# Group norm's sums taken with the residual, x normalised on GpSimd, maxima turned as fp32r, and a plan with landing times

## The chip, the cores and the metric

The kernel runs on one core of one Trainium2 chip. The metric is device time in microseconds (us). Three runs of the kernel before gave 111.69, 111.75 and 113.16 us, median 111.75. One more execution was profiled; all rows below are from it.

## What is computed

The input x has shape 2 x 128 x 16 x 16: a batch of 2, with 128 channels (C) and 256 tokens (T). Four attention blocks run one after the other, and each takes the x that the one before gave:

```
h = group_norm(x, 32 groups of 4 channels x 256 tokens) * gn_w + gn_b
q, k, v = wq h + bq, wk h + bk, wv h + bv
p = softmax(q k^T * scale)        # blocks 0 to 2: 8 heads of 16; block 3: 1 head of 128
x = x + wp (p v) + bp
```

## The kernel before

The whole problem lives in SBUF. Channels are the 128 partitions and tokens the free dimension, so each of the two samples (b = 0 and 1) is one 128x256 tile, `xs0` or `xs1`. The work is cut into steps named (kind, block l, sample b, index i). `step_needs` lists what each step waits for. `plan_order` is a list scheduler: from a table of costs (`STEPS`, `ONE_HEAD_STEPS`), landing times of the first transfers (`LANDED`) and priorities (`LEAD`, `FAVOURED`) it makes one order of all steps and gives each a PSUM bank, of which there are eight. Each engine then runs its own steps in that order, strictly one after the other, and waits on semaphores for the others. So the numbers in the tables decide which instruction stands behind which, and nothing at run time does.

One block of several heads runs like this for each sample:

- Group norm. DVE takes the moments of x (`bn_stats` over 256 tokens, `bn_aggr`, and two operations on one column, L622 to L625). TensorE averages them over the groups (`group_means`, L412 and L414), DVE forms the variance (L630), GpSimd raises it to the power -1/2 (`rsqrt`, L356), and DVE normalises x into `hn` (L633).
- Projections on TensorE: two of q and two of k (each serves a set of four heads, L431) and one of v (L438). ACT and DVE split q and k into parts in fp32r (a format of 32 bits that TensorE takes in one pass, where fp32 needs two instructions): L555, L560, L645, L650. GpSimd extends k (L352).
- Scores in four steps of two heads (`scores`, L451); DVE takes the negative row maxima (`row_max`, L666) into columns of `neg_max`. `turn_max` (L466 and L469) turns a set's maxima into rows by a product with the identity, and ACT stores them in `q_max` (L580).
- Scores again with keys as rows (`scores_t`, L483), `exps` on ACT (L584), `attend` on TensorE (L495), which also gives the sums. ACT stores that (L599), TensorE turns it (`turn_out`, L517), DVE divides (L683, L688), TensorE turns it back (`turn_back`, L525), DVE adds the bias of v (`att`, L661), `project_out` (L532), and DVE adds the residual into `xs` (L701).

Block 3 has one head and half as many operations. Before each block's projections its weights are scaled by gn_w (`scale_w`, L549) and gn_b is folded into the biases (`fold_bias`, ten weight loads with a matmul of one column each, L423 and L424; then `add_bias` on DVE, L640).

The plan also puts fillers on TensorE (`warm`, a 128x128 fp32 product of zeros, L406), where by its own reckoning the engine would do too little in a while. It counts each as 0.222 us, at any time of the program. In the order before there are 24: 16 in the head and 8 at the ends of blocks 0 to 2. The first transfers go out from two queues: SP's has x of sample 0, the weights of block 0, x of sample 1 and then the other weights; ACT's has the constants and the vectors.

The lines of `turn_max`, for the types:

```
mm(dst[:, 0:T], only_high[:, :], q_split[b][:, i, :], start=True, stop=False)          # L466, fp32r
pe.wait_ge(max_done, nth("row_max", l, b, PER * (i + 1) - 1))
for qc in range(NCH):
    last = mm(dst[:, qc * CHUNK:(qc + 1) * CHUNK], neg_max[b][:, i, qc, :], ident, ...)  # L469, fp32
```

Of the kernel before, what the change touches and what calls it, by code (L numbers as in the profile page):

```python
# [46 lines left out]
    "moments": ("V", .95, 1.1), "group_means": ("P", .3, .6), "variance": ("V", .25, .4),  # L47
    "rsqrt": ("G", .56, .65), "normalise": ("V", .4, .6), "project_q": ("P", .43, .65), "project_k": ("P", .43, .65),
    "mask_q": ("A", .47, .65), "split_q": ("V", .41, .6), "round_k": ("A", .4, .56), "split_k": ("V", .41, .6),
    "extend_k": ("G", .7, .8), "project_v": ("P", .45, .65), "store_v": ("A", .32, .5),  # L50
    "scores": ("P", .5, .68), "row_max": ("V", .6, .78), "turn_max": ("P", .57, .8), "store_max": ("A", .32, .5),
    "scores_t": ("P", .5, .68), "exps": ("A", .495, .7), "attend": ("P", .9, 1.1), "store_out": ("A", .32, .5),
    "turn_out": ("P", .25, .45), "divide": ("V", .5, .65), "turn_back": ("P", .25, .45),
    "store_attended": ("V", .41, .6), "project_out": ("P", .5, .7), "residual": ("V", .41, .6),
}
ONE_HEAD_STEPS = {
# [9 lines left out]
LANDED = {("moments", 0, 0, 0): 3.5, ("scale_w", 0, 0, 0): 4.9, ("group_means", 0, 0, 0): 4.4,  # L66
          ("moments", 0, 1, 0): 5.6}
# [4 lines left out]
LEAD = [17, 5, 5, -14]  # L72
FAVOURED = {"attend": -33, "normalise": 26, "exps": -22, "turn_max": 22, "store_out": 35, "scores": -14, "scores_t": -13, "row_max": -13, "store_max": 21}


def cost(step):

    return ONE_HEAD_STEPS.get(step[0], STEPS.get(step[0])) if step[1] == MULTI else STEPS[step[0]]


EMPTIED_BY = {"fold_bias": "add_bias", "group_means": "normalise", "project_q": "split_q", "project_k": "split_k",
              "project_v": "store_v", "turn_max": "store_max", "attend": "store_out", "turn_out": "divide",
              "turn_back": "store_attended", "project_out": "residual"}
EMPTIED_BY_ONE_HEAD = {"fold_bias": "add_bias", "group_means": "normalise", "project_q": "scale_q",
# [78 lines left out]
def plan_order():  # L163
# [18 lines left out]
    while len(done) < len(needs):  # L182
        best = None
        for step in needs:
# [11 lines left out]
            rank = (start, -way(step) - LEAD[l] * (b == 0) - FAVOURED.get(kind, 0.))  # L196
# [3 lines left out]
        engine, busy, later = cost(step)  # L200
        starts[step] = start
        free[engine] = start + busy
# [8 lines left out]
    for step in sorted((s for s in starts if cost(s)[0] == "P"), key=starts.get):  # L211
        t = max(begin + busy for begin, busy, _ in work[-1:])
        while t + WARM <= starts[step] - MARGIN * (warm > 0 and t > 6.):
            active = sum(share * max(0., min(begin + busy, t) - max(begin, t - WINDOW)) for begin, busy, share in work)
            spare = [n for n in range(BANKS)
                     if all(to <= t or begin >= t + 2 * WARM for begin, to in taken[n])]
            if active < ENOUGH * WINDOW and spare:
                filler = "warm", 0, 0, warm
                starts[filler], banks_of[filler] = t, spare[:1]
                work.append((t, WARM, 1.))  # L220
                warm += 1
            t += WARM
        work.append((starts[step], cost(step)[1], ROWS_USED.get(step[0], 1.) if step[1] < MULTI else 1.))
# [3 lines left out]
def attention_blocks(nc: bass.Bass, x, out, vectors, constants, weights):  # L227
# [10 lines left out]
    with ExitStack() as ctx:  # L238
# [17 lines left out]
        minus_half = const[:, HALF_COL:HALF_COL + 1]  # L256
        blank, blank_exp = sb("blank", [C, C]), sb("blank_exp", [C, 1])
        only_high = sb("only_high", [C, C], F32R)

        bn = [sb(f"bn{b}", [C, 6]) for b in range(B)]  # L260
        mom = [sb(f"mom{b}", [C, 5]) for b in range(B)]
        grp = [sb(f"grp{b}", [C, 2]) for b in range(B)]
# [7 lines left out]
        neg_max = [sb(f"neg_max{b}", [C, SETS, NCH, C]) for b in range(B)]  # L270
# [27 lines left out]
        only_high_ready = sem("only_high_ready")  # L298
        vchain = sem("vchain")
        warm_ready = sem("warm_ready")  # L300
# [43 lines left out]
        def _(pool):  # L344
            for b in range(B):
                nc.gpsimd.memset(neg_max[b][:, :, :, :], 0.0).then_inc(max_zeros_ready, 1)
                nc.gpsimd.memset(v_heads[b][:, :, :, :], 1.0).then_inc(v_ones_ready, 1)
            pool.wait_ge(const_in, 16)
            for kind, l, b, i in order:
# [4 lines left out]
                elif kind == "rsqrt":  # L354
                    pool.wait_ge(variance_ready, nth("variance", l, b))
                    nc.gpsimd.tensor_tensor(grp[b][:, 1:2], grp[b][:, 0:1], minus_half,  # L356
                                            ALU.pow).then_inc(rsqrt_ready, 1)

        @block.tensor
        def _(pe):  # L360
            mm = nc.tensor.matmul

            def bank_free(step, j=0):
# [6 lines left out]
                elif emptier[0] == "normalise":  # L370
                    pe.wait_ge(h_ready, nth(*emptier))
# [27 lines left out]
            for step in order:  # L399
# [7 lines left out]
                elif kind == "group_means":  # L407
# [4 lines left out]
                    mm(m[:, 0:3], group_avg, const[:, EPS_COL + 3 * l:EPS_COL + 3 * (l + 1)], start=True, stop=False)  # L412
                    pe.wait_ge(moments_done, nth("moments", l, b))
                    mm(m[:, 0:3], group_avg, mom[b][:, 0:5:2], start=False, stop=True).then_inc(means_done, 1)  # L414
# [46 lines left out]
                elif kind == "turn_max":  # L461
                    if l == b == i == 0:
                        pe.wait_ge(only_high_ready, 1)
# [4 lines left out]
                    for qc in range(NCH):  # L468
                        last = mm(dst[:, qc * CHUNK:(qc + 1) * CHUNK], neg_max[b][:, i, qc, :], ident,  # L469
# [133 lines left out]
        def _(dve):  # L603
# [10 lines left out]
            for step in order:  # L614
                kind, l, b, i = step
                multi = l < MULTI
                if kind == "moments":
                    if l == 0:
                        dve.wait_ge(x_in[b], 16)
                    else:  # L620
                        dve.wait_ge(x_ready, nth("residual", l - 1, b))
                    link(nc.vector.bn_stats(bn[b][:, :], xs[b][:, :]))  # L622
                    link(nc.vector.bn_aggr(mom[b][:, 0:2], bn[b][:, :]))
                    ts(mom[b][:, 2:3], mom[b][:, 0:1], -1.0, None, ALU.mult)
                    stt(out=mom[b][:, 4:5], in0=mom[b][:, 0:1], scalar=mom[b][:, 0:1], in1=mom[b][:, 1:2],  # L625
                        op0=ALU.mult, op1=ALU.add).then_inc(moments_done, 1)
# [4 lines left out]
                elif kind == "normalise":  # L631
# [130 lines left out]
```

## Time and profile before

| | before |
|---|---|
| median of 3 runs | 111.75 us (111.69 to 113.16) |
| the profiled execution: its time | 111.87 us |
| its span, first to last instruction | 110.1 us |
| TensorE busy | 97.5 us, 89% |
| DVE busy | 70.8 us, 64% |
| ACT busy | 55.2 us, 50% |
| GpSimd busy | 13.1 us, 12% |
| mean granted TensorE clock | 0.984 |

The time is 1.8 us more than the span. PE is TensorE's matmuls, PEld its weight loads, POOL is GpSimd, SP the engine that starts most transfers. A matmul's row gives it until its last result is out, and the next begins before that; what one costs in a stream is the distance from one start to the next. An fp32 matmul stands as two instructions in the profile. The average of a busy share mixes the head, where nothing can be computed yet, with the blocks, so the stretches are read one by one.

### The profile page before, as it was taken

Reading aid. Unit: us, or ns where it says so; the run is one execution under the profiler, and the core shown is the slowest. Engines: PE = TensorE matmul, PEld = TensorE weight load, DVE = VectorE, ACT = ScalarE, POOL = GpSimd, SP = SyncE. Lnnn points to the kernel's source line nnn. Section 1 sums busy time; section 2 is a strip of 40 time slices with the busy share of each in tenths; the row PEclk is TensorE's granted clock in tenths of the full one; section 3 lists DMA queues with packets and bytes.
Section 4 is the critical chain, followed back from the end, with each engine's and each line's share of the span. In section 5 each row is a group of like instructions: output and inputs, shape, how many; then the busy total and the mean of one; then the engine's idle time right before and its main releaser. Section 6 shows DMA issues by size and latency. Waiting matters only on the chain.

```text
span 110.1 us, 2481 instructions
## 1 busy us (share of the span) xinstructions
PE 97.5 (89%) x932; PEld 75.3 (68%) x932; DVE 70.8 (64%) x188; ACT 55.2 (50%) x124; POOL 13.1 (12%) x28
## 2 busy tenths in 40 slices
PE   0299999999999689999999978999999988896991
PEld 0299987978664578779857437878886644776860
DVE  0130578998713769988871176899898027677662
ACT  4300075659596107087359840618757892025620
POOL 7000242220000013222000001052200000110000
PEclk9999999999999999999589999999999999999999
DMA  2970000000000000000000000000000000000011
GB/s 63 337 271 5 0 0 6 0 0 0 9 0 0 0 0 6 0 3 0 6 0 0 6 0 0 0 0 0 6 0 0 6 0 0 0 3 0 6 48 48
DMA packets 1739, 2.28 MB, mean 21 GB/s; under 512 B 320, under 2 KB 1216, under 8 KB 1728
## 3 DMA queue, kind: packets, MB, share of 16 engines
q1 hardware_dynamic: 1440, 1.97, 5.4%
q8 instruction: 8, 0.13, 0.5%
q10 hardware_dynamic: 288, 0.16, 0.5%
q14 instruction: 3, 0.02, 0.1%
HBM read 1.86 MB, written 0.26 MB: 19 GB/s over the span
## 4 chain that ended last, share of the span: by engine, by line
PE 76%; ACT 8%; DVE 6%; DMA 3%; issue 3%; ACTq 0%; DVEq 0%
PE ps L431 11%; PE ps L451 10%; PE ps L495 9%; PE ps L483 9%; ACT probs L584 6%; PE ps L406 6%; PE ps L532 5%; PE ps L469 5%; PE ps L423 4%; DMA vec<-in_vectors 3%; PE ps L438 3%; PE ps L466 3%; PE ps L517 2%; ACT o_raw L599 2%; PE ps L503 2%
## 5 line engine op out<-in xcount | busy, mean ns | idle before, releaser
L666 DVE TENSOR_REDUCE neg_max<-ps 128x2 f32<-128x512 f32 x48 | 30.5, 684 | 1.4 <-PE ps L451 1.3
L584 ACT ACTIVATE probs<-ps 128x512 f32<-128x512 f32 x48 | 25.8, 604 | 6.5 <-PE ps L483 6.4
L555 ACT ACTIVATE q_low<-ps,bias_low,const 128x256 fp32r<-128x256 f32 x12 | 6.8, 565 | 23.7 <-PE ps L431 23.6
L431 PE MATMUL ps<-hn,ws 128*128 128x256 f32 x56 | 14.5, 390 | 1.0 <-issue 0.9
L495 PE MATMUL ps<-probs,v_heads 128*32 128x256 f32 x192 | 13.4, 398 | 0.2 <-ACT probs L584 0.2
L483 PE MATMUL ps<-q_split,k_high 32*128 32x256 f32 x96 | 13.0, 330 | 0.1
L451 PE MATMUL ps<-k_high,q_split 32*128 32x256 f32 x96 | 12.2, 337 | 0.1
L431 PEld LDWEIGHTS ps<-hn,ws 128*128 128x128 f32 x56 | 9.8, 189 | 3.2 <-issue 1.7
L356 POOL TENSOR_TENSOR grp<-grp,const 128x1 f32<-128x1 f32 x8 | 4.4, 552 | 61.4 <-DVE grp L630 61.4
L483 PE MATMUL ps<-q_max,k_ext 32*128 32x256 f32 x96 | 11.1, 281 | 0.0
L451 PE MATMUL ps<-k_low,q_split 32*128 32x256 f32 x96 | 10.9, 292 | 0.0
L683 DVE RECIPROCAL rden<-ps 128x8 f32<-128x8 f32 x12 | 2.5, 206 | 13.0 <-PE ps L517 13.0
L483 PEld LDWEIGHTS ps<-q_split,k_high 32*128 32x128 f32 x96 | 8.5, 187 | 3.2 <-issue 1.9
L451 PEld LDWEIGHTS ps<-k_high,q_split 32*128 32x128 f32 x96 | 8.7, 197 | 1.8 <-issue 1.1
L352 POOL TENSOR_SCALAR k_ext<-k_low,const 128x256 fp32r<-128x256 f32 x12 | 6.7, 558 | 23.9 <-DVE k_low L650 23.9
L423 PE MATMUL ps<-vec,w 128*128 128x1 f32 x32 | 5.0, 277 | 4.9 <-DMA vec<-in_vectors 4.9
L406 PE MATMUL ps<-blank 128*128 128x128 f32 x48 | 9.1, 342 | 0.0
L451 PEld LDWEIGHTS ps<-k_low,q_split 32*128 32x128 f32 x96 | 8.9, 202 | 0.0
L483 PEld LDWEIGHTS ps<-q_max,k_ext 32*128 32x128 f32 x96 | 8.6, 190 | 0.0
L495 PEld LDWEIGHTS ps<-probs,v_heads 128*32 128x32 f32 x192 | 5.2, 113 | 4.8 <-issue 1.7
L423 PEld LDWEIGHTS ps<-vec,w 128*128 128x128 f32 x32 | 4.7, 225 | 5.2 <-DMA vec<-in_vectors 4.9
L406 PEld LDWEIGHTS ps<-blank 128*128 128x128 f32 x48 | 8.0, 250 | 0.0
(61 smaller groups left out, 147.5 us busy)
## 6 DMA issues: line engine op xcount, KB each, us to landing
w<-in_w SPq DMA_DIRECT2D x3, 384.0 KB, 5.2
xs<-in_x SPq DMA_DIRECT2D x2, 128.0 KB, 3.1
w<-in_w SPq DMA_DIRECT2D x1, 256.0 KB, 5.8
out<-xs SPq DMA_DIRECT2D x4, 64.0 KB, 1.5
const<-in_constants ACTq DMA_DIRECT2D x1, 136.0 KB, 2.9
vec<-in_vectors ACTq DMA_DIRECT2D x1, 16.0 KB, 3.7
```

The source lines that it names most:

```text
L352: nc.gpsimd.tensor_scalar(k_ext[b][:, i, :], k_low[b][:, i, :].bitcast(F32), high_rows, one_row, ALU.mult, ALU.add).then_inc(k_extended, 1)
L406: mm(slot(*step)[:, 0:C], blank[:, :], blank[:, :], start=True, stop=True)
L423: mm(dst[:, at + s:at + s + 1], w[l][:, first + s * multi, :], beta, start=True, stop=True)
L431: mm(slot(*step)[:, 0:T], ws[l][:, block_of[l] + i, :], hn[b][:, :], start=True, stop=True).then_inc(done, 1)
L451: last = mm(slot(*step, j)[:, qc * T:(qc + 1) * T], q_split[b][r:r + QUAD, s, qc * CHUNK:(qc + 1) * CHUNK], keys[b][r:r + QUAD, s, :], sta ...
L469: last = mm(dst[:, qc * CHUNK:(qc + 1) * CHUNK], neg_max[b][:, i, qc, :], ident, start=False, stop=(qc == NCH - 1))
L483: last = mm(slot(*step, j)[:, kc * T:(kc + 1) * T], part[b][r:r + QUAD, s, keys], queries[b][r:r + QUAD, s, :], start=(n == 0), stop=(n == 1))
L495: last = mm(slot(*step)[QUAD * j:QUAD * (j + 1), 0:T], v_heads[b][:, kc, h, :], probs[b][:, h, kc, :], start=(kc == 0), stop=(kc == NCH - 1))
L532: mm(slot(*step)[:, 0:tokens], w[l][:, W_P[l], :], att[b][:, i * CHUNK:i * CHUNK + tokens], start=True, stop=True).then_inc(out_projected, 1)
L555: nc.scalar.activation(q_low[b][:, i, :], slot("project_q", l, b, i)[:, 0:T], ACT.Identity, bias=bias_low[:, l, i:i + 1], scale=low_rows). ...
L584: nc.scalar.activation(probs[b][:, i, :, :].rearrange("p c t -> p (c t)"), slot("scores_t", l, b, i // PACK, i % PACK)[:, :], ACT.Exp, sca ...
L666: nc.vector.tensor_reduce(neg_max[b][:, i // PER, :, QUAD * (i % PER) + MAX_ROW], slot("scores", l, b, i // PACK, i % PACK)[:, :].rearrang ...
```

## The change

**Sums in place of moments.** `bn_stats` and `bn_aggr` go, with the two operations on one column. The residual's instruction now also sums x along the tokens (`accum_out`), and one more pass squares x and sums the squares. For block 0, where no residual stands ahead, a first pass sums x. The division by 4 x 256 moves into the constant `group_avg`; a matmul of one column with `minus_avg` (made on GpSimd once) gives the negative mean. So the group's mean, its negative and the mean square stand in the same three PSUM columns as before.

**Normalising on GpSimd.** DVE copies the mean out of PSUM behind the variance (`mean_ready`), and GpSimd normalises x right behind its own rsqrt. The PSUM bank is free once the mean is copied.

**Maxima in fp32r.** `neg_max` and the identity (`ident_r`) are fp32r, so L469's product is one instruction instead of two.

**The plan.** It has new costs and priorities for every kind, its own landing times, and reckons TensorE's steps (fillers too) at twice their cost until 6.5 us. In this early stretch it fills every gap. The whole order follows from that.

```diff
+COLD_UNTIL = 6.5
-LEAD = [17, 5, 5, -14]
-FAVOURED = {"attend": -33, "normalise": 26, "exps": -22, ...
+LEAD = [896.5, -85.3, -422.8, -819.6]
+FAVOURED = {"add_bias": 112.1, "attend": -105, "divide": -244.4, "exps": -68, ...
+def cost_at(step, start):
+    engine, busy, later = cost(step)
+    cold = busy if engine == "P" and start < COLD_UNTIL else 0.
+    return busy + cold, later + cold
...
-        while t + WARM <= starts[step] - MARGIN * (warm > 0 and t > 6.):
+        while True:
+            spent = WARM * (2 if t < COLD_UNTIL else 1)
+            if t + spent > starts[step] - MARGIN * (t > COLD_UNTIL):
+                break
...
-            if active < ENOUGH * WINDOW and spare:
+            if (t < COLD_UNTIL or active < ENOUGH * WINDOW) and spare:
...
+                elif kind == "normalise":
+                    pool.wait_ge(rsqrt_ready, nth("rsqrt", l, b))
+                    pool.wait_ge(mean_ready, nth("variance", l, b))
+                    nc.gpsimd.tensor_scalar(hn[b][:, :], xs[b][:, :], grp[b][:, 1:2], grp[b][:, 2:3],
+                                            ALU.subtract, ALU.mult).then_inc(h_ready, 1)
...
+                    mm(m[:, 1:2], minus_avg[:, :], mom[b][:, 0:1], start=False, stop=False)
                     pe.wait_ge(moments_done, nth("moments", l, b))
-                    mm(m[:, 0:3], group_avg, mom[b][:, 0:5:2], start=False, stop=True).then_inc(means_done, 1)
+                    mm(m[:, 0:3], group_avg, mom[b][:, :], start=False, stop=True).then_inc(means_done, 1)
...
-                        last = mm(dst[:, qc * CHUNK:(qc + 1) * CHUNK], neg_max[b][:, i, qc, :], ident,
+                        last = mm(dst[:, qc * CHUNK:(qc + 1) * CHUNK], neg_max[b][:, i, qc, :], ident_r[:, :],
...
+                        link(stt(out=squares[b][:, :], in0=xs[b][:, :], scalar=0.0, in1=xs[b][:, :], op0=ALU.mult,
+                                 op1=ALU.add, accum_out=mom[b][:, 0:1]))
...
-                    link(nc.vector.bn_stats(bn[b][:, :], xs[b][:, :]))
-                    link(nc.vector.bn_aggr(mom[b][:, 0:2], bn[b][:, :]))
-                    ts(mom[b][:, 2:3], mom[b][:, 0:1], -1.0, None, ALU.mult)
-                    stt(out=mom[b][:, 4:5], in0=mom[b][:, 0:1], scalar=mom[b][:, 0:1], in1=mom[b][:, 1:2],
-                        op0=ALU.mult, op1=ALU.add).then_inc(moments_done, 1)
+                    stt(out=squares[b][:, :], in0=xs[b][:, :], scalar=1.0, in1=xs[b][:, :], op0=ALU.mult,
+                        op1=ALU.mult, accum_out=mom[b][:, 2:3]).then_inc(moments_done, 1)
...
-                elif kind == "normalise":
-                    dve.wait_ge(rsqrt_ready, nth("rsqrt", l, b))
-                    ts(hn[b][:, :], xs[b][:, :], slot("group_means", l, b)[:, 0:1], grp[b][:, 1:2], ALU.subtract,
-                       ALU.mult).then_inc(h_ready, 1)
+                    ts(grp[b][:, 1:2], m[:, 0:1], 1.0, None, ALU.mult).then_inc(mean_ready, 1)
```

The order of instructions moves on every engine; two places of TensorE's order show how. In these rows `blank` marks a filler, `vec,w` is `fold_bias`, `const` and `mom` are `group_means`, and `hn,ws` or `ws,hn` are the projections. The first place is the head of TensorE's program, here in the kernel before.

```order
L423 MATMUL ps<-vec,w 128x1 x4
L424 MATMUL ps<-vec,w 128x1
L406 MATMUL ps<-blank 128x128 x10
L412 MATMUL ps<-const 128x3
L414 MATMUL ps<-mom,const 128x3
L406 MATMUL ps<-blank 128x128 x6
```

After the last of these rows there is a second pair of L412 and L414 for sample 1, and then the first projection. This is the same place in the changed kernel.

```order
L438 MATMUL ps<-blank 128x128 x8
L444 MATMUL ps<-const 128x3
L450 MATMUL ps<-mom,minus_avg 128x1
L452 MATMUL ps<-mom,const 128x3
L461 MATMUL ps<-vec,w 128x1 x4
L462 MATMUL ps<-vec,w 128x1
L469 MATMUL ps<-hn,ws 128x256 x4
```

The fillers now stand ahead of all else, eight of them. Sample 0's means come before `fold_bias`, and between that and the projections nothing is left; sample 1's means have moved behind the projections of sample 0.

The second place is the end of block 0. Here `probs,v_heads` is `attend` for one set of four heads, `o_raw` is `turn_out`, `o_tok` is `turn_back`, and `att,w` is `project_out`. TensorE's rows of the kernel before, from the last `attend` of sample 1 to the first projections of block 1:

```order
L495 MATMUL ps<-probs,v_heads 32x256 x8
L532 MATMUL ps<-att,w 128x256
L517 MATMUL ps<-const,o_raw 128x128 x4
L412 MATMUL ps<-const 128x3
L414 MATMUL ps<-mom,const 128x3
L406 MATMUL ps<-blank 128x128
L525 MATMUL ps<-const,o_tok 128x128 x2
L406 MATMUL ps<-blank 128x128 x2
L532 MATMUL ps<-att,w 128x256
L431 MATMUL ps<-hn,ws 128x256 x4
```

And of the changed kernel, from the last `attend` of sample 1 to the first scores (`k_high,q_split`) of block 1:

```order
L533 MATMUL ps<-probs,v_heads 32x256 x8
L555 MATMUL ps<-const,o_raw 128x128 x4
L469 MATMUL ps<-hn,ws 128x256 x2
L563 MATMUL ps<-const,o_tok 128x128 x2
L469 MATMUL ps<-hn,ws 128x256 x2
L476 MATMUL ps<-ws,hn 128x128 x2
L570 MATMUL ps<-att,w 128x256
L489 MATMUL ps<-k_high,q_split 128x256 x2
```

Sample 0's `project_out` and means have moved ahead of these rows, in among the second scores and the `attend` steps of sample 1. Block 1's projections for sample 0 now surround sample 1's `turn_back` and `project_out` instead of following them. There are no fillers in this place; four stand later in block 1, ahead of sample 1's projections. The ends of blocks 1 and 2 moved in the same way but less: only one projection goes ahead of sample 1's `project_out`, and it stands behind `turn_back`. Altogether the changed order has 12 fillers.

## Rows read from the trace of the kernel before

**Rows 1.** The page: busy time of each engine, share of the span, instructions

```profile
PE 97.5 (89%) x932; PEld 75.3 (68%) x932; DVE 70.8 (64%) x188; ACT 55.2 (50%) x124; POOL 13.1 (12%) x28
```

**Rows 2.** Windows: stretch, length, busy PE PEld DVE ACT POOL, granted clock, DMA, GB/s

```profile
0.00:13.54 13.54, 8.64 (x51) 8.64 (x51) 3.05 (x14) 2.31 (x3) 2.67 (x9) 1.00 0.42 137
13.54:34.63 21.09, 20.61 (x238) 15.69 (x237) 15.22 (x33) 15.38 (x34) 2.79 (x5) 1.00 0.01 2
34.63:40.41 5.78, 4.36 (x37) 3.19 (x38) 3.59 (x13) 0.66 (x3) 0.55 (x1) 1.00 0.00 0
40.41:64.15 23.74, 23.24 (x244) 17.51 (x243) 16.75 (x38) 15.61 (x34) 2.74 (x5) 0.93 0.01 2
64.15:68.83 4.68, 4.04 (x35) 2.65 (x35) 3.37 (x12) 0.40 (x2) 0.55 (x1) 1.00 0.00 0
68.83:91.22 22.39, 22.03 (x244) 16.90 (x243) 16.65 (x38) 15.51 (x34) 2.74 (x5) 1.00 0.01 1
```

**Rows 3.** The chain of waits in the head: start us, us, what

```profile
1.16 3.69 DMA vec<-in_vectors
...
4.90 1.86 PE ps L423 x8
6.76 0.43 PE ps L424 x2
7.19 4.34 PE ps L406 x20
...
11.87 1.44 PE ps L406 x12
```

**Rows 4.** The timeline of the head: start us, us, engine, line, operation, [idle before]

```profile
0.72 0.38 SPq L330 DMA_DIRECT2D xs<-in_x  x1
0.82 0.17 DVE L612 MEMSET blank<- 128x128 f32 x1 [0.82 <-PEq L756]
...
11.91 0.29 DVE L630 TENSOR_SCALAR grp<-ps 128x1 f32<-128x1 f32 x1 [3.40 <-PE ps L414]
...
12.35 0.56 POOL L356 TENSOR_TENSOR grp<-grp,const 128x1 f32<-128x1 f32 x1 [9.72 <-DVE grp L630]
```

**Rows 5.** The tile xs: issue to landing of its two loads, least, median, most

```profile
DMA to landing us min/median/max: 2.7/3.1/3.4
```

**Rows 6.** The chain at the end of block 0: start us, us, what

```profile
35.76 0.64 PE ps L532 x2
...
38.88 0.42 PE ps L525 x2
```

**Rows 7.** Groups by form: busy us, mean ns of one, idle before

```profile
L352 POOL TENSOR_SCALAR k_ext<-k_low,const 128x256 fp32r<-128x256 f32 x12 | 6.7, 558 | 23.9 <-DVE k_low L650 23.9
L599 ACT ACTIVATE o_raw<-ps 128x256 f32<-128x256 f32 x12 | 4.8, 398 | 5.9 <-PE ps L495 5.9
L701 DVE SCALAR_TENSOR_TENSOR xs<-ps,vec,xs 128x256 f32<-128x256 f32 x6 | 2.9, 483 | 2.8 <-PE ps L532 2.8
L589 ACT ACTIVATION_READ_ACCUMULATOR p_one<-ps,neg_max_one 128x1 f32 x4 | 0.8, 196 | 0.0
```

**Rows 8.** The timeline of TensorE at one turn_max

```profile
29.80 0.39 PE L466 MATMUL ps<-q_split,only_high 128*128 128x256 f32 x1
30.02 0.61 PE L469 MATMUL ps<-const,neg_max 128*128 128x128 f32 x4
30.47 0.38 PE L517 MATMUL ps<-const,o_raw 128*128 128x128 f32 x2
```

**Rows 9.** Windows in block 1: TensorE busy, and its granted clock ahead of DMA

```profile
52.00:53.00 1.00, 1.00 (x16) 0.88 (x19) 0.96 (x4) 0.89 (x3) 0.00 (x0) 0.61 0.00 0
...
55.00:56.00 1.00, 1.00 (x16) 0.28 (x8) 1.00 (x3) 0.65 (x2) 0.00 (x0) 0.69 0.00 0
```

**Rows 10.** Two attend steps, block 1 and block 0: start us, us

```profile
28.18 1.00 PE ps L495 x16
...
54.53 1.55 PE ps L495 x16
```

## The prediction: what the change should do to the time

> **What bounds the kernel now.** I read the busy table first: TensorE is busy 89% of the span and nobody else over 64% [rows 1]. That is an average, so I cut the span with the windows view at the places where the program changes character [rows 2]. The reader should see three kinds of stretch. The head lasts 13.54 us and ends with the first projection. A block has an inner stretch of 21.1 to 23.7 us, from its first projection to its last exponential, in which TensorE is busy 98% and DVE and ACT some 70%. Between blocks lie 4.7 to 5.8 us in which TensorE has fillers and gaps: the last attend of sample 1 has to become x again, and that takes every engine in turn. The stretch between blocks 2 and 3 is as long as the one between 1 and 2, 4.68 us.
>
> Then the chain of waits in the head [rows 3]. It waits for the vectors until 4.85, runs `fold_bias` from 4.90 to 7.19 (1.86 and 0.43) and then goes through 20 instructions of fillers in 4.34 us. [...] The plan believed 0.222 each and put ten in front of sample 0's means. x of sample 0 had landed at 0.72 + 2.7 = 3.4 us [rows 4, 5]. So some 4 us of the head is filler that real work waited behind, and DVE too had put the bias ahead of the moments. The head is this kernel's largest single loss.
>
> **Part 1, the head.** The changed order has eight fillers first. They can start when `blank` is set, at 0.82 + 0.17 = 0.99 [rows 4], and end at 0.99 + 8 x 0.434 = 4.46. DVE's two passes over x of sample 0 start at 3.4. No row shows a summing pass of DVE with both inputs in SBUF. The nearest is the residual, the same operation on 128x256, 0.48 us; ACT's accumulator costs 0.20 more in an instruction of its own [rows 7]. So a pass is 0.48 to 0.68; I take 0.48, and the moments are there at 4.5 (4.9 at the upper end). Sample 0's means are three small matmuls of two instructions; none is dearer than a filler's two, 0.43. The last of them stands behind the moments, so the means are there at about 5.3. From there two things run side by side. [...] On the other side, variance to the start of rsqrt is 12.35 - 11.91 = 0.44, rsqrt 0.56 [rows 4], normalising on GpSimd 0.56 by the one operation of its form and size there, `k_ext` [rows 7], and about 0.15 for each of the hops: 5.3 + 0.44 + 0.56 + 0.56 + 0.3 = 7.2. [...] First projection 7.2 to 7.6, at worst 8.0; I take 7.5 against 13.54: **-6.0 us**. The scaled weights are no obstacle: ACT needs under a microsecond after the vectors' 4.85.
>
> Sample 1's two passes stand in DVE's order ahead of the bias; its x took 3.4 us from issue to landing [rows 5], so they too are done before `fold_bias` is.
>
> **Part 2, the end of block 0.** Before, from the last exponential to the next projection it takes 5.78 us [rows 2]. `project_out` of sample 0 stands behind the last attend, at 35.76 [rows 6], so DVE gets sample 0's residual and moments just when sample 1's divisions should start, and `turn_back` starts only at 38.88. In the changed order `project_out` of sample 0 goes ahead, among the second scores. The path left is attend 1.00 [rows 10], ACT's store 0.40 [rows 7], `turn_out` 0.38 [rows 8] and two hops, 0.2: first projection after about 2.0. But `turn_back` (0.42) and `project_out` (0.64) of sample 1 [rows 6] now run inside block 1, and its four fillers, 0.24 each [rows 3], show that sample 1's norm comes late there. I count them in full, 1.0. 5.8 - 2.0 - 1.06 - 1.0 = **-1.8 us** with the rounding (5.78, 0.96).
>
> **Part 3, the ends of blocks 1 and 2.** Here sample 1's tail keeps its serial path through `turn_back` and `project_out`, and only sample 0's norm is out of its way: a shorter chain on DVE, and one projection ahead of `project_out`. From 4.68 I take off 0.3 each: **-0.6 us**. The bound below is nothing; above, that of part 2.
>
> **Part 4, the maxima in fp32r.** One `turn_max` takes 0.22 (one fp32r instruction of 256 columns) and then 0.45 for four fp32 instructions of 128 columns, start to start [rows 8]. Two are left. No row shows an fp32r product of 128 columns with 128 rows. If each costs as much as the one of 256 columns, 0.22, nothing is saved; if as much as one fp32 pass, 0.11, 0.23 is saved; if half of that, 0.34. I take 0.23 (the loads of 128 rows are still there), so 12 x 0.23 = 2.8 us of TensorE's time. Inside a block TensorE is busy 98%, but DVE and ACT, at 15 to 17 us of 21 to 24 [rows 2], limit in parts, where the gain turns into waiting. I count 0.7 of it: **-2.0 us**, bounds 0 and -4.1.
>
> **Part 5, the rest at nothing.** DVE loses the moments' four operations and the normalising, and gains a squaring pass and a copy of one column, under 0.3 as the variance's is [rows 4]. The difference relieves DVE a little, which TensorE's busy 98% hides; if that cover is gone, it is a gain. `group_means` gains two small instructions, 0.1 us each eight times, partly in gaps. GpSimd has 12% load [rows 1], so eight more of 0.56 find room; what is queued behind them is `extend_k`, which is needed only after the first maxima.
>
> **Sum.** The profiled execution took 111.87, its span 110.1; the median of the runs, 111.75, is the same within 0.1%. 111.9 - 6.0 - 1.8 - 0.6 - 2.0 = **101.5 us**. I keep the one stretch at the lower clock in block 1 (below) as it is.
>
> **A rule against the change.** In this trace `k_ext` on GpSimd takes 558 ns at each of its twelve places, while DVE works alongside, and no DVE operation of size there reads two inputs from SBUF [rows 7]. The new squaring passes do, and they can meet a normalising. If a normalising had to wait for one whole pass each time, up to 0.48 us eight times would be lost, of which the first is covered by `fold_bias`. [...] No row here shows it either way. Most squaring passes stand in DVE's order ahead of the norm that waits for them, so they meet the other sample's `k_ext` rather than a normalising.
>
> **Rivals.**
> - *Only the head.* The new order's ends of blocks bring nothing, because sample 1's tail is just moved into the next block, and the fp32r product is no cheaper. Then 111.9 - 6.0 = 105.9. For it speaks that I have not seen an fp32r product of this shape. Against it, the gaps between blocks are there in the windows.
> - *The lock.* GpSimd's normalising waits for DVE as above: 101.5 + 3.4 = 104.9.
> - [...] In block 1 the granted clock falls between 52 and 56 us [rows 9], and the same sixteen instructions of attend take 1.55 instead of 1.00 [rows 10]. The mean of 0.93 over 23.74 us [rows 2] makes that 1.7 us. Before it TensorE did scores on 32 rows and the one-column matmuls of `fold_bias`. The change halves the fillers, from 24 to 12, and thins `turn_max`. Two more such stretches give 101.5 + 3.4 = 104.9. Without any it would be 99.8, and with TensorE's full saving of part 4 it would be 97.7.
> [...]
> - *The change does nothing*, because the fillers ahead of the real work were covering a late transfer. x at 3.4 and the vectors at 4.85 exclude that for the head.
>
> **How the numbers follow.** The forecast 0.58, only the head 0.12, the lock 0.08, more stretches at 1.2 GHz 0.10, a better one (no lower clock, the full saving of part 4) 0.08, the two last rivals together 0.04. The range goes from 97.7, the better case, to 105.5, which takes in the lock and two more stretches at the lower clock; "only the head" and the last two stay outside, 0.16. A measurement of this kernel can tell some 2% from no change, that is 109.5 to 114.0. The last two rivals, at about 112, are nearly all "same": faster 0.96, same 0.03, slower 0.01.
>
> **What would show it.** In the profile after: first projection at 7.2 to 7.6 us (part 1); from the last exponential of block 0 to block 1's first projection about 2 us, and that of blocks 1 and 2 still 3.9 to 4.4 (parts 2, 3); the product of `neg_max` at about 0.11 an instruction, start to start, two instead of four (part 4); normalising at 0.56 on GpSimd, without outliers (the lock); one stretch with a granted clock under 1 (the clock). The prediction is wrong if the first projection stands later than 8.5, or if the inner stretches grow by what the ends lost.

## The result, and the profile after

| | before | changed |
|---|---|---|
| median of 5 runs | 111.75 us | 113.35 us (113.06 to 117.56) |
| ratio, 95% interval | | 1.0135 [1.0098, 1.0172] |
| span, profiled execution | 110.1 us | 113.4 us |
| DVE busy | 70.8 us | 67.1 us |
| GpSimd busy | 13.1 us | 23.9 us |
| mean granted TensorE clock | 0.984 | 0.925 |

The forecast was 101.5 us, in a range from 97.7 to 105.5. The changed kernel is 1.4% slower than before. The executions scatter: three lie near 113, and the profiled one, which all lines below are from, took 115.34 at nearly the same mean clock (0.925 against 0.923), so no trace shows what the 2 us between them are.

Two lines of the changed kernel's page. The second gives the granted clock in 40 slices of the span (9 is full speed, 5 is half); before, all but two slices showed 9:

```profile
PE 99.3 (88%) x900; PEld 76.5 (67%) x900; DVE 67.1 (59%) x183; ACT 55.5 (49%) x124; POOL 23.9 (21%) x39
PEclk9999985999999999999999999997555999995999
```

The windows of the changed kernel, cut at the same events as [rows 2] (columns as there) and carried on through the end of block 2 and block 3. For the last two, the kernel before has these:

```profile
91.22:95.90 4.68, 3.82 (x34) 2.43 (x34) 3.37 (x12) 0.39 (x2) 0.55 (x1) 1.00 0.00 0
95.90:110.10 14.20, 10.75 (x61) 8.34 (x59) 8.79 (x29) 4.90 (x16) 0.55 (x1) 1.00 0.07 20
```

And the changed kernel:

```profile
0.00:8.59 8.59, 6.99 (x32) 6.93 (x33) 2.89 (x15) 2.31 (x3) 4.78 (x13) 1.00 0.65 217
8.59:35.09 26.50, 24.53 (x238) 19.21 (x238) 16.50 (x37) 15.82 (x34) 3.99 (x6) 0.94 0.01 2
35.09:38.13 3.04, 2.45 (x26) 1.40 (x26) 1.24 (x6) 0.72 (x3) 1.78 (x2) 1.00 0.00 0
38.13:61.06 22.93, 21.71 (x248) 16.66 (x248) 16.81 (x40) 14.95 (x34) 3.99 (x6) 1.00 0.01 2
61.06:65.52 4.46, 2.69 (x28) 1.69 (x29) 2.65 (x11) 0.67 (x3) 1.78 (x2) 1.00 0.01 4
65.52:92.36 26.84, 25.25 (x238) 18.63 (x238) 15.99 (x37) 15.10 (x34) 3.97 (x6) 0.81 0.01 1
92.36:96.81 4.45, 2.73 (x30) 1.69 (x29) 2.68 (x11) 0.66 (x2) 1.78 (x2) 1.00 0.00 0
96.81:113.40 16.59, 12.96 (x64) 10.33 (x64) 8.35 (x28) 5.24 (x16) 1.78 (x2) 0.90 0.06 16
```

The head did give 4.95 us (13.54 to 8.59) and the end of block 0 2.7. The two other ends gave 0.2 each. But block 0's inner stretch grew from 21.1 to 26.5, block 2's from 22.4 to 26.8, and block 3 from 14.2 to 16.6; only block 1's became shorter, by 0.8. In the blocks TensorE is busy 93 to 95% in place of 98%, and the granted clock in block 2 is 0.81.

The groups by form show the instruction at fault, of the changed kernel (L388 normalises, L379 is `k_ext`):

```profile
L388 POOL TENSOR_SCALAR hn<-xs,grp 128x256 f32<-128x256 f32 x8 | 9.9, 1232 | 0.8
L379 POOL TENSOR_SCALAR k_ext<-k_low,const 128x256 fp32r<-128x256 f32 x12 | 6.6, 555 | 15.7 <-DVE k_low L686 15.7
```

Same engine, same size, both a `tensor_scalar` with two operations: 1.23 us against 0.56. The chain of the changed kernel shows who waits for it, and what comes then (L469 are projections, L504 and L507 `turn_max`):

```profile
8.46 0.14 issue
8.59 3.75 PE ps L469 x8
...
14.81 1.23 POOL hn L388
16.05 0.09 issue
16.14 2.63 PE ps L469 x6
...
22.33 0.32 PE ps L504
22.64 0.17 PE ps L507 x2
```

The first eight projection instructions take 3.75 us; in the kernel before the same eight took 1.84. In x0_forms below the same eight took 3.75 where the record gives a granted clock of 0.50 (8.54 to 12.30), so 3.75 is the time at half the full clock, though the record of the changed kernel says 1.00 there. From 15.0 to 16.1 TensorE stands still for sample 1's normalising, and the next six take 2.63. The windows around that stop, of the changed kernel:

```profile
15.00:16.00 1.00, 0.01 (x1) 0.00 (x0) 1.00 (x3) 0.00 (x0) 1.00 (x1) 1.00 0.00 0
16.00:17.00 1.00, 0.86 (x3) 0.78 (x4) 1.00 (x3) 0.00 (x0) 0.04 (x1) 0.71 0.00 0
17.00:18.00 1.00, 1.00 (x4) 0.82 (x3) 1.00 (x2) 0.47 (x1) 0.00 (x0) 0.50 0.00 0
```

### The profile page after: what moved, and what is told of

The parts are those of the page before. It is cut to its first block, busy times and chain, and to the rows that moved or that the text cites. A ratio compares the mean times of both kernels' runs of the same rounds, so it can differ in the third digit from the quotient of the medians.

```text
span 113.4 us, 2434 instructions
## 1 busy us (share of the span) xinstructions
PE 99.3 (88%) x900; PEld 76.5 (67%) x900; DVE 67.1 (59%) x183; ACT 55.5 (49%) x124; POOL 23.9 (21%) x39
## 3 DMA queue, kind: packets, MB, share of 16 engines
q1 hardware_dynamic: 1440, 1.97, 5.2%
HBM read 1.86 MB, written 0.26 MB: 19 GB/s over the span
## 4 chain that ended last, share of the span: by engine, by line
PE 79%; issue 6%; ACT 6%; POOL 3%; DVE 3%
PE ps L469 16%; PE ps L533 11%; PE ps L489 10%; PE ps L521 10%; ACT probs L622 5%; PE ps L438 4%; PE ps L476 4%; PE ps L570 4%; PE ps L555 2%; PE ps L504 2%; POOL hn L388 2%; PE ps L461 2%; PE ps L452 2%; PE ps L541 2%; PE ps L497 2%
## 5 line engine op out<-in xcount | busy, mean ns | idle before, releaser
L702 DVE TENSOR_REDUCE neg_max<-ps 128x2 fp32r<-128x512 f32 x48 | 30.0, 685 | 8.1 <-PE ps L489 8.1
L469 PE MATMUL ps<-hn,ws 128*128 128x256 f32 x56 | 19.1, 479 | 7.0 <-issue 5.3
L469 PEld LDWEIGHTS ps<-hn,ws 128*128 128x128 f32 x56 | 12.2, 235 | 10.1 <-issue 8.5
L598 ACT ACTIVATE k_high<-ps,bias 128x256 fp32r<-128x256 f32 x12 | 5.5, 474 | 22.7 <-PE ps L469 22.7
L489 PE MATMUL ps<-k_high,q_split 32*128 32x256 f32 x96 | 11.9, 335 | 0.5 <-ACT probs L622 0.3
L521 PE MATMUL ps<-q_split,k_high 32*128 32x256 f32 x96 | 10.8, 344 | 1.2 <-ACT q_max L618 1.1
L388 POOL TENSOR_SCALAR hn<-xs,grp 128x256 f32<-128x256 f32 x8 | 9.9, 1232 | 0.8
L379 POOL TENSOR_SCALAR k_ext<-k_low,const 128x256 fp32r<-128x256 f32 x12 | 6.6, 555 | 15.7 <-DVE k_low L686 15.7
L637 ACT ACTIVATE o_raw<-ps 128x256 f32<-128x256 f32 x12 | 4.7, 393 | 10.4 <-PE ps L533 10.4
L521 PE MATMUL ps<-q_max,k_ext 32*128 32x256 f32 x96 | 9.4, 293 | 0.0
L686 DVE SCALAR_TENSOR_TENSOR k_low<-ps,bias,k_high 128x256 fp32r<-128x256 f32 x12 | 5.4, 480 | 3.4 <-ACT k_high L598 3.4
L697 DVE TENSOR_SCALAR att<-ps,bias 128x256 f32<-128x256 f32 (+1 forms) x10 | 4.3, 430 | 4.7 <-PE ps L563 3.7
```

The source lines that it names most:

```text
L379: nc.gpsimd.tensor_scalar(k_ext[b][:, i, :], k_low[b][:, i, :].bitcast(F32), high_rows, one_row, ALU.mult, ALU.add).then_inc(k_extended, 1)
L388: nc.gpsimd.tensor_scalar(hn[b][:, :], xs[b][:, :], grp[b][:, 1:2], grp[b][:, 2:3], ALU.subtract, ALU.mult).then_inc(h_ready, 1)
L469: mm(slot(*step)[:, 0:T], ws[l][:, block_of[l] + i, :], hn[b][:, :], start=True, stop=True).then_inc(done, 1)
L489: last = mm(slot(*step, j)[:, qc * T:(qc + 1) * T], q_split[b][r:r + QUAD, s, qc * CHUNK:(qc + 1) * CHUNK], keys[b][r:r + QUAD, s, :], sta ...
L521: last = mm(slot(*step, j)[:, kc * T:(kc + 1) * T], part[b][r:r + QUAD, s, keys], queries[b][r:r + QUAD, s, :], start=(n == 0), stop=(n == 1))
L598: nc.scalar.activation(k_high[b][:, i, :], slot("project_k", l, b, i)[:, 0:T], ACT.Identity, bias=bias[:, l, K_BIAS + i:K_BIAS + i + 1]).t ...
```

## The experiments

Times are medians of four executions with their range, and the kernel before on the same chip beside them. Different groups of variants ran on different chips. The theory: the subtract form on GpSimd is slow, and the stops that it causes and the fp32r product lower the clock. The rivals: the new order itself, and the removed fillers.

### What a tensor_scalar costs on GpSimd

```diff
 # abridged
+ for op0, op1 in (subtract, mult), (add, mult), (mult, add), (mult, subtract), (mult, mult), ...
+     nc.gpsimd.tensor_scalar(probe, hn[0], one_row, high_rows, op0, op1)   # unused, one after the other
```

> The changed kernel with ten more tensor_scalar operations on GpSimd after its last normalising, each on 128 partitions with per-partition scalars, waiting for one another: subtract then mult, add then mult, mult then add, mult then subtract, mult then mult (256 columns, fp32 out), subtract then mult and mult then add with fp32r out, a single mult, and subtract then mult and mult then add on 128 columns. They compute nothing that is used. Theory (the pair of operations sets GpSimd's price): the mult-then-add forms take 0.55 us like k_ext, and those that begin with subtract 1.22, whatever the output type. Rival (the operand sets it, since the normalising reads scalars from a tile just written, or its output is fp32): all forms with fp32 output take 1.22, or all of them 0.55. On 128 columns a slow form should cost about 0.65, since the price goes with the columns.

The timeline of GpSimd in this kernel, the second, third and fourth form:

```profile
107.43 0.55 POOL L410 TENSOR_SCALAR probe<-hn,const 128x256 f32<-128x256 f32 x1
108.08 0.56 POOL L410 TENSOR_SCALAR probe<-hn,const 128x256 f32<-128x256 f32 x1
108.73 1.23 POOL L410 TENSOR_SCALAR probe<-hn,const 128x256 f32<-128x256 f32 x1
```

Subtract then mult took 1.25 and mult then subtract 1.23; add-mult, mult-add and mult-mult 0.55 to 0.56. A subtract in either place doubles the price. With fp32r output subtract-mult took 1.23 and mult-add 0.67; `k_ext`, which is such a mult-add, takes 0.56, so that difference stays open. A single mult took 0.93, more than two operations. On 128 columns it was 0.80 against 0.45: I had expected 0.65 for the slow form, and the price does not halve with the columns. The whole kernel took 120.71 in this one execution. That is not the probes' time: they end at 115.2 beside block 3, the chain that ended last does not go through them, and the granted clock was 0.841.

### The normalising on DVE, and on GpSimd with an add

```diff
-nc.gpsimd.tensor_scalar(hn, xs, mean, rstd, ALU.subtract, ALU.mult)
+nc.vector.tensor_scalar(hn, xs, mean, rstd, ALU.subtract, ALU.mult)          # x1_dve
+nc.gpsimd.tensor_scalar(hn, xs, minus_mean, rstd, ALU.add, ALU.mult)         # x4_add; the copy takes column 1
```

> The changed kernel with the normalising back on DVE, at the same place of the same order. [...] Rival (the clock falls because fillers were taken out, not because of the gaps): 108 to 110 with a granted clock of still about 0.92. Rival (the new order is bad inside the blocks): 109 or more with a high clock.

> The changed kernel with one form exchanged: the copy takes the negative mean out of PSUM, and GpSimd normalises with add and mult in place of subtract and mult. Same result, same order. Theory (the subtract form is what made the normalising 1.23 us; add then mult took 0.55 in the probe): eight normalisings of 0.56, time like the one with the normalising on DVE or a little under, 103 to 106 us, the path shorter by 0.67 at five to seven of them and the clock lower less often. [...]

On DVE: 106.48 (104.52 to 107.23) against 112.63, ratio 0.934 [0.922, 0.946]; I had expected 102 to 106. With the add on GpSimd: 106.44 (104.33 to 106.67) against 112.01. The changed kernel itself has 113.35 against 111.75. The eight normalisings of the second, by its line:

```profile
L388 POOL TENSOR_SCALAR hn<-xs,grp x8: 553/554/618, 7.2 to 93.7; 128x256 f32<-128x256 f32 x8
```

One ALU name is worth 7 us of 113.4. Eight times 0.67 us are only 5.4, and not all of that is on the path; the granted clock also rose, to 0.967 to 0.984 from 0.92. How the 7 us divide between the two is not measured. Which engine normalises does not matter (106.48 and 106.44).

The mean granted clock is not the whole account either. On DVE the two executions at 1.00 took 107.0 and 107.2, and those at 0.984 and 0.967 took 105.9 and 104.5. In the profiled one (107.23) TensorE's durations are still the long ones until after 13.5 us (eight instructions of `fold_bias` in 1.85, eight of the projections in 3.76), where the record shows 1.00; the others have no trace.

### Fillers where TensorE waits

```diff
# four fillers ahead of each sample's first projection in each block, one ahead of the first of all
+if step[0] == "project_k" and step[3] == 0:
+    order.append(filler)
```

> The changed kernel, with four fillers ahead of each sample's first projection in each block (one in the first place), 29 more in all, in the bank of that projection. They stand where TensorE waits for the normalising. Theory (TensorE's clock falls because TensorE stands still there): the granted clock rises from 0.92 to 0.97 or more, and the time falls by 3 to 5 us, to 108 to 110, though every normalising is as slow as before. Rival (the clock does not hang on these gaps): granted clock stays at 0.92, time same or up to 2 us longer.

110.9, between 107.41 (clock 0.984) and 115.45 (0.895), against 112.63; ratio 0.958 [0.946, 0.969]. I had expected 108 to 110 at 0.97 or more. The two best executions, 107.41 and 108.43, had clocks of 0.984 and 1.00 and are 5 to 6 us under the changed kernel with every normalising as slow as before. None of the changed kernel's nine executions was above 0.939. So the clock can be had back by work where TensorE stops, and the slow form alone, with the clock high, costs little: 107.41 against 106.44 with the add. But the two others, 113.37 (0.939) and 115.45, gained nothing, so the fillers there do not secure the clock.

### The head alone, and fp32r maxima in it

```diff
 # the kernel before, with new landing times only (x3_head, x11_head_again)
-LANDED = {("moments", 0, 0, 0): 3.5, ..., ("group_means", 0, 0, 0): 4.4, ("moments", 0, 1, 0): 5.6}
+LANDED = {("moments", 0, 0, 0): 3.7, ..., ("fold_bias", 0, 0, 0): 4.9, ("moments", 0, 1, 0): 5.7}
 # and in addition (x7_head_r)
-mm(dst[...], neg_max[b][:, i, qc, :], ident, ...)
+mm(dst[...], neg_max[b][:, i, qc, :], ident_r, ...)      # both fp32r
 # and in addition (x10_r_fill): one filler ahead of each turn_max
```

> The kernel before with nothing changed but the plan's landing times, so that fillers come first, sample 0's means come ahead of fold_bias, and the moments ahead of the bias: the head alone. [...] Rival (an earlier start only runs into the lower clock, and gives it back): under 2 us gained.

> The head-only variant once more, on the chip of the others here, since it was measured on another chip than its fp32r version. Theory: 105 to 108, granted clock 0.97 or more, as before, so the 9.5 us between the two are the fp32r maxima. Rival (the difference was the chip): 113 or so here.

> The head-only variant of the kernel before (new landing times only), with the maxima written and turned as fp32r in addition, in the same order. Theory (0.28 us less in each of twelve turn_max steps, most of them on the path): 1.5 to 3 us under the head-only variant's 105.6, so 102.6 to 104. Rival (inside the blocks DVE and ACT hold the path): under 0.5 us, 105 or more; or the clock falls more often because TensorE has less to do.

> The head-only variant with fp32r maxima, which took 113.2 to 117.3 at a granted clock of 0.87, with one filler (two fp32 instructions of 128 columns, 0.22 us) ahead of each of the twelve turn_max steps. That puts back roughly the TensorE time that fp32r had saved, in another place and with useless work. Theory (the clock hangs on how much TensorE does, and fp32r took it below what it takes): clock back to 0.96 or more and 105 to 108. Rival (fp32r products themselves, or their type, lower the clock): 113 or more, granted clock below 0.9.

| | us | before | ratio | granted clock |
|---|---|---|---|---|
| x3_head | 105.62 (105.36 to 107.9) | 112.63 | 0.936 [0.929, 0.944] | 0.965 to 0.983 |
| x11_head_again | 106.11 (105.84 to 106.39) | 112.18 | 0.949 [0.945, 0.953] | 0.983 to 0.984 |
| x7_head_r | 115.01 (113.2 to 117.25) | 112.01 | 1.016 [1.005, 1.026] | 0.852 to 0.874 |
| x10_r_fill | 107.07 (106.64 to 107.24) | 112.18 | 0.957 [0.953, 0.961] | 0.966 to 0.967 |

The head alone takes off 6 to 7 us, more than the 4 to 5 that I expected here and about what part 1 said. Adding fp32r maxima, with all else in place, adds 9; twelve fillers that do nothing useful take 8 of these back. So it is not the fp32r products as such that lower the clock. Of x3_head, three windows:

```profile
10.00:14.50 4.50, 4.50 (x46) 3.50 (x44) 4.19 (x9) 3.06 (x7) 1.22 (x3) 1.00 0.00 0
14.50:17.80 3.30, 3.08 (x35) 2.59 (x34) 3.10 (x7) 1.47 (x4) 0.39 (x2) 1.00 0.02 5
17.80:27.80 10.00, 9.85 (x144) 6.95 (x143) 6.11 (x14) 8.34 (x20) 0.50 (x1) 1.00 0.01 2
```

And the same of x7_head_r, its fp32r version:

```profile
10.00:14.50 4.50, 4.50 (x46) 3.51 (x45) 4.33 (x9) 3.06 (x7) 1.34 (x3) 1.00 0.00 0
14.50:17.80 3.30, 3.26 (x36) 2.71 (x37) 3.30 (x7) 1.47 (x5) 0.67 (x2) 1.00 0.02 5
17.80:27.80 10.00, 10.00 (x100) 7.24 (x100) 5.30 (x12) 6.55 (x15) 0.19 (x1) 0.50 0.01 2
```

The two run alike until 14.5 us. Then come two `turn_max` steps, 0.28 us shorter each, and scores on 32 rows; from 17.8 on the second has a granted clock of 0.50 for 10 us and starts 100 matmuls where the first starts 144. Between 14.5 and 17.8 the second was busy 3.26 us of 3.30, more than the first with 3.08, so a stop is not what lowered its clock. It fell in all four executions (0.852 to 0.874 as a mean) and not in those of x10_r_fill, which put fp32 work back. So the clock can fall without a stop, where fp32 work is taken out. Whether fillers in fp32r would hold it as well was not tried.

With the fillers of x10_r_fill the granted clock was 0.966 in place of 0.87. But work without a stop did not always bring the clock up: in x13_full_r below TensorE was busy for all of 1.04 to 13.57 us, and from 10.37 on its eight projection instructions still took 3.43 us, for 1.85 in the chains of x3_head and x10_r_fill.

### Maxima back in fp32 in the changed kernel

> The changed kernel with GpSimd's normalising in the add-then-mult form and the maxima back in fp32 (two products of four instructions), same order. Compared with the same kernel with fp32r maxima (106.44, 104.3 to 106.7). Theory (the faster product costs the clock more than it saves): the clock stays at 0.98 or more in all executions and the time is no longer, 103 to 106, though TensorE has 12 x 0.28 = 3.4 us more to do. Rival (in this order the work is dense enough for fp32r, only the other order suffers): 107 to 109.

> The changed kernel with only the maxima back in fp32; the normalising stays slow. Theory (fp32r maxima share in the changed kernel's low clock): granted clock above 0.95 instead of 0.92, time 109 to 112. Rival (the gaps from the slow normalising alone pull the clock down): clock still about 0.92, and 114 to 116, by the 3.4 us of work added.

With the fast normalising: 105.17 (104.03 to 108.06) against 106.44 with fp32r, 1.3 us less, within the scatter, though TensorE has 3.4 us more to do. The clock did not stay at 0.98 in all executions, as I had expected: it was 0.936 to 1.00. With the slow one: 113.05 (110.14 to 118.5) against 112.18 before. Its two best, 110.1 and 110.3, give the ratio 0.985 [0.980, 0.991] at a clock of 0.969, and its two others took 115.8 and 118.5 at 0.925 and 0.912; the changed kernel has 111.53 to 119.19 over all its executions. So in the new order fp32r maxima save nothing that can be measured. That they share in the changed kernel's miss is likely by the best executions, but not shown; in any case they cost far less there than the 9 us of the old order.

### The clock in the head

```diff
 # in words; the first fillers stand ahead of sample 0's means, the others ahead of the first projection
+x5_eleven, x6_both (with the add): three more fillers at the start
+x12_full, x13_full_r (with the add; maxima fp32 and fp32r): one more at the start, four ahead of the projection
```

> The changed kernel with three more fillers in its head, eleven instead of eight, and nothing else. [...] Rival (the clock in the head is a matter of phase and not of the fillers' number): no change, 113.

> The changed kernel with both: add and mult on GpSimd, and eleven fillers in the head. [...] Rival (the new order also loses inside the blocks): 104 or more with a granted clock above 0.97.

> The kernel with add-then-mult on GpSimd and fp32 maxima (105.17 before), with one more filler at the start (nine) and four ahead of the very first projection, where TensorE stood still for 1.0 us. [...]

> The same fillers with fp32r maxima. Theory: as the one with fp32 maxima or up to 2 us less, since TensorE has 3.4 us less to do, 101 to 104, but with a lower granted clock in some executions. Rival (fp32r maxima cost clock in this order too): 105 or more, granted clock under 0.96.

> The changed kernel itself, on the chip of these two, since the variants were measured on other chips than it. All theories expect 113 to 118 with a granted clock of 0.92; a time under 110 would mean that the variants' gains were partly the chip's.

Eleven fillers alone did not help: 116.32 (114.19 to 120.17) for the changed kernel, where I had expected 109 to 111, and 106.24 (105.54 to 113.42) with the add, the same as with eight and not the 101 to 103 expected. x12_full took 104.64 (102.44 to 106.72) against 111.57, expected 102 to 103.5. Eight instructions of its `fold_bias` took 0.89 us, where the chain of the kernel before has 1.86; its chain:

```profile
1.04 4.21 PE ps L451 x18
...
5.98 0.89 PE ps L474 x8
```

What the fillers in the stop did is seen beside x8_add_f32, the same kernel without them and with one filler fewer at the start. TensorE's timeline of x8_add_f32, `fold_bias` and then the first projections:

```profile
5.27 1.03 PE L461 MATMUL ps<-vec,w 128*128 128x1 f32 x8
6.16 0.36 PE L462 MATMUL ps<-vec,w 128*128 128x1 f32 x2
7.44 3.57 PE L469 MATMUL ps<-hn,ws 128*128 128x256 f32 x8 [0.91 <-POOL hn L388]
```

And of x12_full:

```profile
5.84 1.03 PE L474 MATMUL ps<-vec,w 128*128 128x1 f32 x8
6.74 0.36 PE L475 MATMUL ps<-vec,w 128*128 128x1 f32 x2
6.96 1.14 PE L451 MATMUL ps<-blank 128*128 128x128 f32 x8
8.01 1.97 PE L482 MATMUL ps<-hn,ws 128*128 128x256 f32 x8
```

In both, eight instructions of `fold_bias` took 1.03 us; in the changed kernel they took 1.84. After the stop of 0.91 us the eight projection instructions take 3.57, at a granted clock of 0.53 (7.44 to 11.02), and with fillers in its place 1.97; I had expected about 1.85. Three more profiles of the new order (x0_forms, x6_both, x9_f32) had `fold_bias` in 1.03 and then a stop, of 0.91 to 1.58 us; their projections took 2.82 to 3.75. But the whole kernel gained only 0.5 us by it, within the scatter.

x13_full_r took 108.34 (102.89 to 113.4), expected 101 to 104. In its profile TensorE worked without a stop from 1.04 us on, and the first projections still took 3.43, for 1.85 in the chain of x3_head:

```profile
6.32 1.71 PE ps L474 x8
8.03 0.43 PE ps L475 x2
8.45 1.92 PE ps L451 x8
10.37 3.43 PE ps L482 x8
```

So in these profiles filling the stop kept a clock that had risen, and did not make it rise. When it rises is not settled: in the four profiles of the old order with the new head it had risen ahead of `fold_bias`, by 5.3 to 6.2 us (`fold_bias` took 1.03 for eight instructions); in the new order in five profiles of twelve, with nearly the same instructions at the start. In the other seven `fold_bias` took 1.84 or 1.85 and the first projections 3.62 to 3.76, in some with no stop between them. The changed kernel itself gave 114.2 (111.53 to 119.19) on this chip, against 111.57; the chip is not the reason.

## Why the prediction was wrong, step by step

- **The signs.** I had named two signs of being wrong, and both came: the first projection stands at 8.59, later than 8.5, and the inner stretches of blocks 0 and 2 grew by 5.4 and 4.5, more than the ends lost.
- **What bounds the kernel, and the head: right.** The two head-only runs gave -7.0 and -6.1 for the predicted -6.0. In the changed kernel the first projection came at 8.59, outside the 7.2 to 8.0. The fillers ended at 4.82 for 4.46, and the three small matmuls ran behind them one after the other, so the means were there at 5.9 and not at 5.3; and the normalising took 1.29 for 0.56. The passes of DVE were well sized: 0.43, and 0.08 for the sum. The 7.6 at the upper end of my sum is the 5.3 and `fold_bias` at its 2.29 of before: it took 2.27 in the changed kernel (5.75 to 8.02), and 1.26 in x12_full (5.84 to 7.10).
- **The step that failed: "normalising on GpSimd 0.56 by the one operation of its form and size there".** The form was not the same. `k_ext` is a mult and an add, the normalising a subtract and a mult, and that is 1.23. This term should have come from a row for the same pair of operations, or been open upwards. Part 5 then called eight of them free. With the add in place of the subtract the kernel takes 106.44 in place of 113.35, so this step holds 7 of the 11.9 us missed, with what it did to the clock.
- **The rival on the clock was mis-sized.** I named it by a frequency, which no run here shows; what the runs show of such a stretch is a granted clock of 0.50 (x7_head_r, 17.80 to 27.80). I gave it 0.10, and priced two more stretches at 1.7 us each. By the mean of 0.925 over 113.4 us the changed kernel lost an estimated 8.5 us of full clock, before 1.8 (0.016 of 110.1). The head comes on top, where the record says 1.00 and eight projection instructions took 1.9 us too long. This overlaps with the step above: the slow form's stops are one cause of it. I saw that fillers and fp32 work were taken out and did not ask what the old fall in [rows 9] had hung on.
- **Part 4: the size right, the sign wrong.** Two instructions in 0.17 for four in 0.45 save 0.28 each, inside the bounds. But the time did not fall by it: +9 in the old order, by way of the clock, and in the new one no gain (106.44 against 105.17 without it), where I had -2.0.
- **Part 2 and 3: the mechanism right, the gain mostly absent.** 3.0 us from the last exponential to the first projection of block 1, 4.5 for the others. The 0.67 too much per normalising is in both; with the fast form x12_full has 2.4 and 3.8, for the predicted 2.0 and 3.9 to 4.4. But beside x3_head, with the old order and the new head, x12_full's profile is only 1.0 us shorter (102.7 against 103.7): the three ends are shorter by 5.1 together, the inner stretches longer by 1.8, the head by 0.7 and block 3 by 1.7 (15.9 against 14.2). Block 3 was at nothing in my sum. Its granted clock is 0.89 in x12_full and 0.90 in the changed kernel. By an estimate, 0.11 of 15.9 us is 1.7, the whole growth.
- **"Only the head" is nearly what came, once the faults are out.** I gave it 0.12, at 105.9. By the medians, head-only took 0.938 and 0.946 of the time of the kernel before on its chip, and x8_add_f32 and x12_full 0.938 both. The new order thus brings 1 us at most beyond its head, where I had -2.4 for parts 2 and 3.
- **The lock: its case did not arise.** In the trace no squaring pass ran beside a normalising. Two ran beside sample 0's rsqrt in the head (6.20 to 7.08), and it took 0.74 for 0.56, 0.2 more and not a whole pass. The first normalising took 1.29 for 1.22, but beside DVE's `only_high` and `ident_r`, which read one tile. What a normalising would lose beside such a pass, no run here shows; the whole pass of 0.48 each, 3.4 us in all, was my estimate.
- **The last two rivals: the number near by chance.** I had put them at about 112, and 113.35 came. But the head did give 4.95 us, and block 0's inner stretch had a granted clock of 0.94, so TensorE was not at half the full clock all through it.

With the add, fp32 maxima and the fillers in the head, x12_full has a median of 104.64 and a best of 102.44. That is inside the range, but 3 us above the forecast: 2.0 of them are part 4, which is not in x12_full, and about as much is what block 3 lost by the clock. Why the clock falls there is open.

## What to carry to other kernels

Take the price of an operation from a row with the same ALU operations, not only the same engine and size; where there is none, probe it. In a kernel whose TensorE is the bound, do not count less work on it as a gain in itself (x7_head_r, with less of it, took 115.01 for x3_head's 105.62): look at the granted clock around the places where work is removed, and keep fillers there until a run shows that they can go. The safest version here is the kernel before with new landing times, 105.4 to 107.9 over eight executions. The best single execution is x12_full's, 102.44, but its median against the kernel before is the same, 0.938.

## What the hardware did that I had not expected

- On GpSimd a tensor_scalar with a subtract took 1.22 to 1.25 us for 128x256 in fp32, with add and mult in any order 0.55 to 0.56, and a single mult 0.93 (x0_forms).
- TensorE's granted clock fell to 0.50 with its busy share at 0.99 to 1.00 (x7_head_r, 17.80 to 27.80), after nothing but 0.56 us of fp32 work was taken out of the stretch ahead.
- In four profiles where eight instructions of `fold_bias` took 1.03 us in the head and TensorE then stood still for 0.91 to 1.58 us, its next eight instructions took 2.82 to 3.75 us; with fillers in the stop they took 1.97 (x12_full).
- In the head its instructions kept their long durations through 12 us of uninterrupted work in one execution (x13_full_r: 1.84 for eight of `fold_bias` at 6.18, 3.43 for the projections from 10.37), and had the short ones at about 5 us in others (x8_add_f32 and x9_f32: 1.03 for eight of `fold_bias` at 5.27).
